# Edge sources and lanes read once in the mean pass of a four-layer graph network, instead of turn by turn

## The chip, the cores and the metric

The kernel runs on one core of a Trainium2 chip. The metric is the device time of one execution in microseconds (us), lower is better. A core has five engines with their own instruction streams: TensorE (PE in the profile, with its weight loads as PEld), VectorE (DVE), ScalarE (ACT), GpSimd (POOL) and SyncE (SP). They meet only at semaphores. SP and ACT issue plain DMAs, POOL issues the indirect ones (gathers).

## The reference

Four graph layers are applied in turn to `x`, 6,250 nodes of 96 numbers, over the same 200,000 edges, each with a source `src`, a target `dst` (the edges come sorted by `dst`), 32 attributes (`edge_attr_32`) and 17 attributes (`edge_attr_17`). Each layer adds its result to `x` and reads `h = relu(layernorm(x))`.

```
L0  out[d]  = mean over edges into d of (h[src] @ W + b)
L1  in      = [h[src], attr32];  msg = gelu(in@mW1+mb1)@mW2+mb2;  gate = sigmoid(gelu(in@gW1+gb1)@gW2+gb2)
    agg[d]  = sum of msg*gate;   out = layernorm(h + gelu([h,agg]@uW1+ub1)@uW2+ub2)
L2  w       = relu(attr17@W1.T+b1)@W2.T+b2;   agg[d] = sum of w*h[src];   out = relu(h@Ws.T+bs+agg@Wn.T+bn)
L3  three graph convolutions with degree-normalised sums, between two dense layers
```

## The kernel before

Nodes lie in 49 blocks of 128 (`NB`). The first stages bring the edges into a sorted form in the chip's memory and build a dense count matrix (`adjacency`); L0 (the mean pass, `mean_layer`) and L3 (`graph_layers`) multiply with it. L1 and L2 run through the edges themselves in `edge_pass`, once as `"gated"` (L1) and once as `"filter"` (L2). The change is about these two edge passes.

An edge tile is 128 consecutive edges of one node block. There are `T` = 1,612 of them, handled `G` = 4 at a time: a pass is `Q` = 403 turns. Rings have `GPI` = 6 slots of one turn each. For a turn the pass needs the first sorted row of each tile (`tile_row`, one number per tile), the (source, target) pairs of its 512 edges (`sorted_pairs` in HBM, `pairs_h`), their attributes (`sorted_attr`), and the node rows of the sources, gathered from `node_rows_wide` (192 numbers, gated) or `node_rows` (96 numbers, filter).

The function `turns` writes out the order of an engine by hand: every engine gets a list of (work, lag), and in its iteration n it does each work of turn n minus lag, in the order of the list. A program loop holds six iterations.

In the gated pass:

- SP (`load`, L1850s): waits until the consumers are done with the slot (`rows_used`, `src_kept`, `fields`: turn n-6), reads four row numbers into registers and issues four DMAs of pairs into `idx_ring` (L1858).
- POOL (`gather`, L1883): waits for the pairs (`idx_ready`), then issues four indirect DMAs into `rows`.
- ACT: `tanh` of turn n-5 (L1977), `gelu` of n-4 (L1972), `keep` of n-4 (L1982: copies the sources to `src_all`, for the filter pass), and then `load_attributes` of n: four row numbers and four DMAs into `attr_ring` (L1839).
- DVE: `dots` of n-3 (L2012), `combine` of n-2 (L2003, the only reader of the gathered `rows`), `gates` of n-3 (L2019), `turn_attrs` of n (L1995), and `hots_and_adds`: for turn n-3 it subtracts `tile_node` from the targets (L1907, gives `lane_all`), makes four one-hot tiles `hots` (L1917), and between them adds the four sums of turn n-4 into `accT` (L1926).
- PE: `edge_part` of n-1 (L1959), `sum_targets` of n-3 (L1932).

In the filter pass SP issues one DMA for the sources (`src_all` to `idx_ring`, L1861) and four for attributes (L1839); POOL gathers as before; PE does transposes of the attributes (`ps_t`, L1941, lag 0), `layer1` (`ps_e`, L2033, lag 1), `layer2` (`ps_w`, L2040, lag 2) and `sum_targets` (L1932, lag 4); ACT `keep_attrT` (L1948, lag 0) and `relu` (L2051, lag 1); DVE hots (L1920, lag 4) and adds (L1926, lag 5) and then `times` (L2060, lag 3, the only reader of `rows`).

PE and DVE depend on each other in each turn: `sum_targets` needs the one-hots (semaphore `hot`), the adds and the next one-hots need the sums (`summed`).

## Time and profile before

| | before |
|---|---|
| median of 3 runs | 8719.87 us (8703.91 to 8736.1) |
| the profiled execution, its own time | 8702.86 us |
| its span, first to last instruction | 8701.0 us |
| lies around the span | 1.9 us |
| mean granted TensorE clock | 0.749 of full speed |
| busy: PE / DVE / POOL / ACT | 67% / 50% / 37% / 20% |

The profile is one execution. "Busy" counts an engine's own work, not its register, branch and semaphore instructions or the issue of a DMA by SP or ACT; a gather counts as busy on POOL. An idle time is put down to what released it; "remote" and "issue" stand where no recorded instruction could be named as the releaser. Start times in a timeline are counted from the start of the span.

### The profile page before, as it was taken

Reading aid. Unit: us, or ns where it says so; the run is one execution under the profiler, and the core shown is the slowest. Engines: PE = TensorE matmul, PEld = TensorE weight load, DVE = VectorE, ACT = ScalarE, POOL = GpSimd, SP = SyncE. Lnnn points to the kernel's source line nnn. Section 1 sums busy time; section 2 is a strip of 40 time slices with the busy share of each in tenths; the row PEclk is TensorE's granted clock in tenths of the full one; section 3 lists DMA queues with packets and bytes.
Section 4 is the critical chain, followed back from the end, with each engine's and each line's share of the span. In section 5 each row is a group of like instructions: output and inputs, shape, how many; then the busy total and the mean of one; then the engine's idle time right before and its main releaser. Section 6 shows DMA issues by size and latency. Waiting matters only on the chain. (4 is left out here: it accounts for less than half of the span.)

```text
span 8701.0 us, 138050 instructions
## 1 busy us (share of the span) xinstructions
PE 5807.8 (67%) x29615; PEld 4088.1 (47%) x29617; DVE 4309.2 (50%) x14738; ACT 1723.7 (20%) x3202; POOL 3183.4 (37%) x3326
## 2 busy tenths in 40 slices
PE   4313666784455455555554688888888788889999
PEld 4312344663333333333332455555555555677777
DVE  7877888335666666666666333333333333332222
ACT  0013888101111111111111111111111111110000
POOL 0101000005555555555552455555555555300000
PEclk9956888897777777777777656655665666689999
DMA  1231333653333333333332211111111111256666
GB/s 31 101 100 60 105 106 107 215 180 77 68 71 69 70 70 67 71 69 70 71 70 31 42 34 35 34 35 34 35 34 34 33 36 35 24 188 252 249 243 221
DMA packets 1067041, 756.40 MB, mean 87 GB/s; under 512 B 870578, under 2 KB 979842, under 8 KB 1035091
## 3 DMA queue, kind: packets, MB, share of 16 engines
q1 hardware_dynamic: 679714, 476.62, 18.5%
q0 software_dynamic: 131296, 241.31, 10.9%
q10 hardware_dynamic: 255904, 37.09, 2.5%
q8 instruction: 43, 0.70, 0.0%
q14 instruction: 84, 0.68, 0.0%
HBM read 651.15 MB, written 141.61 MB: 91 GB/s over the span
## 5 line engine op out<-in xcount | busy, mean ns | idle before, releaser
L1883 POOL DMA_INDIRECT rows<-node_rows,idx_ring x1612 | 1529.2, 949 | 1215.1 <-DMA idx_ring<-src_all 702.5
L1883 POOL DMA_INDIRECT rows<-node_rows_wide,idx_ring x1612 | 1544.0, 958 | 1149.5 <-DMA idx_ring<-sorted_pairs 634.5
L1932 PE MATMUL ps_sum<-hots,act_ring 128*97 128x128 f32 x3224 | 657.8, 369 | 1326.6 <-DVE hots L1917 621.1
L1920 DVE TENSOR_SCALAR hots<-iota,lane_all 128x128 f32<-128x128 f32 x1612 | 461.6, 287 | 1820.4 <-remote 1283.4
L1932 PEld LDWEIGHTS ps_sum<-hots,act_ring 128*97 128x97 f32 x3224 | 556.7, 234 | 1618.9 <-DVE accT L1926 1235.1
L1932 PE MATMUL ps_sum<-hots,msg 128*96 128x128 f32 x3224 | 724.4, 399 | 419.0 <-DVE hots L1920 212.6
L1389 PE MATMUL ps_conv<-conv_rows,adj_ring 128*128 128x288 bf16 x7350 | 919.1, 287 | 29.8 <-PEq L1765 16.2
L1926 DVE TENSOR_TENSOR accT<-accT,ps_sum 97x128 f32 (+1 forms) x3224 | 905.8, 281 | 37.0 <-issue 16.0
L1932 PEld LDWEIGHTS ps_sum<-hots,msg 128*96 128x96 f32 x3224 | 624.9, 258 | 449.9 <-DVE accT L1926 360.2
L1959 PE MATMUL ps_e<-w1e,aT 128*128 128x384 f32 x1612 | 814.7, 642 | 18.3 <-DVE aT L1995 15.9
L1389 PEld LDWEIGHTS ps_conv<-conv_rows,adj_ring 128*128 128x128 f16 x7350 | 721.6, 98 | 212.1 <-issue 18.2
L2040 PEld LDWEIGHTS ps_w<-w2w,hid 97*128 97x128 f32 x3224 | 577.6, 269 | 516.1 <-issue 475.2
L2033 PE MATMUL ps_e<-aT,w 18*96 18x512 f32 x806 | 656.5, 906 | 55.6 <-ACT aT L1948 34.6
L2040 PE MATMUL ps_w<-w2w,hid 97*128 97x96 f32 x3224 | 661.5, 370 | 22.7 <-issue 12.0
L1125 DVE TENSOR_TENSOR end_hot<-iota_h,lanes 128x3072 bf16<-128x3072 bf16 x350 | 602.8, 1756 | 144.8 <-PE ps_blocks L1149 142.8
L1149 PE MATMUL ps_blocks<-end_hot 128*128 128x256 bf16 x2800 | 493.1, 323 | 256.3 <-POOLq L1196 191.2
L1948 ACT ACTIVATE aT<-ps_t 18x512 f32<-18x512 f32 x403 | 235.6, 585 | 2034.1 <-remote 1567.5
L1917 DVE TENSOR_SCALAR hots<-iota,lane_all,gate 128x128 f32<-128x128 f32 x1612 | 564.5, 352 | 17.1 <-issue 1.3
L1149 PEld LDWEIGHTS ps_blocks<-end_hot 128*128 128x128 bf16 x2800 | 304.0, 109 | 446.1 <-issue 347.6
L1977 ACT ACTIVATE th<-z,half_gb 128x4 f32<-128x4 f32 x403 | 119.8, 297 | 1897.6 <-remote 918.5
L1959 PEld LDWEIGHTS ps_e<-w1e,aT 128*128 128x128 f32 x1612 | 380.9, 261 | 195.4 <-issue 141.3
L2003 DVE TENSOR_TENSOR act_ring<-ps_e,rows 128x384 f32<-128x384 f32 x806 | 413.2, 548 | 64.5 <-issue 34.6
(345 smaller groups left out, 5907.2 us busy)
## 6 DMA issues: line engine op xcount, KB each, us to landing
adj_ring<-adjacency SPq DMA_DIRECT2D x240, 1280.0 KB, 5.5
adjacency<-panels SPq DMA_DIRECT2D x588, 128.0 KB, 1.7
attr_ring<-sorted_attr ACTq DMA_DIRECT2D x1612, 16.0 KB
idx_ring<-sorted_pairs SPq DMA_DIRECT2D x1612, 1.0 KB
rows<-node_rows_wide,idx_ring POOLq DMA_INDIRECT x1612
attr_ring<-sorted_attr SPq DMA_DIRECT2D x1612, 8.5 KB
rows<-node_rows,idx_ring POOLq DMA_INDIRECT x1612
sorted_attr<-in_edge_attr SPq DMA_DIRECT2D x5, 5000.0 KB
```

The costliest lines, as they stand in the source:

```text
L1125: v.tensor_tensor(end_hot[:, r, n * PAIRS:(n + 1) * PAIRS, :, :, :] .rearrange("p t c l k -> p (t c) l k"), iota_h[:, :, :].unsqueeze(1).t ...
L1149: pe.matmul(ps_b[:, dyn(at[j], WD)], src_hot[:, r, j // 2, :, j % 2], dst_hot[:, r, j // 2, :, j % 2], start=False, stop=True, skip_group_ ...
L1389: last = pe.matmul(ps[:, d, 0:width], ring[:, c, s * cols + d * P:s * cols + (d + 1) * P], nodes[:, c * CB + s, 0:width], start=(c == 0 an ...
L1883: g.indirect_dma_start(out=rows[:, r, j, 0:width], out_offset=None, in_=table, in_offset=bass.IndirectOffsetOnAxis(ap=idx, axis=0)).then_i ...
L1917: last = v.tensor_scalar(hots[:, r % 2, j, :], iota[:, :], lane, gate[:, r % 3, j:j + 1], ALU.is_equal, ALU.mult)
L1920: last = v.tensor_scalar(hots[:, r % 2, j, :], iota[:, :], lane, None, ALU.is_equal)
L1926: v.tensor_tensor(acc, acc, ps_sum[0:M, ra % 2, j, :], ALU.add).then_inc(added.sem, 1)
L1932: last = pe.matmul(ps_sum[0:M, r % 2, j, :], what(r, j), hots[:, r % 2, j, :], start=True, stop=True)
L1959: last = pe.matmul(ps_e[:, r % 2, c, 0:4 * D], aT[:, r % 2, :], w1e[:, 2 * c:2 * c + 2, :].rearrange("p j d -> p (j d)"), start=True, stop ...
L2003: last = v.tensor_tensor(act_ring[:, r % 3, 2 * c:2 * c + 2, :, 0:D].rearrange("p j a d -> p (j a) d"), ps_e[:, r % 2, c, 0:4 * D].rearran ...
L2033: pe.matmul(ps_e[0:D, r % 2, :], w17[:, :], aT[:, r % 2, :], start=True, stop=True).then_inc(edge_mm.sem, 1)
L2040: last = pe.matmul(ps_w[:, r % 2, j, 0:D], hid[:, r % 2, j * P:(j + 1) * P], w2w[:, :], start=True, stop=True)
```

## The change

Near the end of the mean pass the pairs of all 1,612 tiles are brought on chip once. SP spreads `tile_row` (padded to 13 x 128) over the partitions (`tile_at`), POOL gathers for each of 13 columns 128 tiles' pairs, 1 KB per tile (`pair_rows`), ACT casts them to float, PE turns them with 13 transposes for the sources and 13 for the targets, and ACT copies these out of PSUM to `src_all` and `lane_all` (four copies each). A DVE instruction in the stage that stores the wide rows turns `lane_all` into lanes for all tiles at once.

In both edge passes `idx_ring` is then filled by ACT: a new first work `take_sources` (lag 0) waits until the gathers of turn n-6 have landed and copies the turn's four columns of `src_all`. POOL waits for this copy and, itself now, for `rows_used`. SP issues attribute loads alone in both passes; the pair DMAs, the source DMAs, `keep`, `load_attributes` on ACT and the lane subtraction per turn are gone. In the filter pass the lags of all PE, ACT and DVE works grow by one.

```diff
@@ mean_layer @@
                 def _(sp):
+                    sp.dma_start(tile_at[:, :], tile_row[:, :].rearrange("o (p k) -> o p k", k=TC))\
+                        .then_inc(tile_at_in.sem, 16)
                     load_adjacency(sp, ring, 0, range(1, NK))
+                    sp.wait_ge(tile_at_in.sem, 16)
                 def _(g):
                     gather_heavy(g, heavy_rows)
+                    g.wait_ge(tile_at_in.sem, 16)
+                    for k in range(TC):
+                        g.indirect_dma_start(out=pair_rows[:, k, :], out_offset=None, in_=pairs_h,
+                                             in_offset=bass.IndirectOffsetOnAxis(ap=tile_at[:, k:k + 1], axis=0))\
+                            .then_inc(pairs_in.sem, 16)
+                @block.scalar
+                def _(a):
+                    a.wait_ge(pairs_in.sem, 16 * TC)
+                    a.activation(pair_rows[:, :, :].bitcast(F32).rearrange("p k e -> p (k e)"),
+                                 pair_rows[:, :, :].rearrange("p k e -> p (k e)"), ACT.Copy).then_inc(pairs_cast.sem, 1)
+                    for c, t in enumerate((src_all, lane_all)):
+                        by_run = t[:, :].rearrange("p (t n) -> p n t", n=TC)
+                        for n, (first, runs) in enumerate(quads):
+                            a.wait_ge(pairs_turned.sem, c * len(quads) + n + 1)
+                            a.activation(by_run[:, first:first + runs, :],
+                                         ps_p[:, n, 0:runs * P].rearrange("p (k t) -> p k t", t=P),
+                                         ACT.Copy).then_inc(pairs_kept.sem, 1)
                 def _(pe):
+                    def turn_pairs(c):
+                        for n, (first, runs) in enumerate(quads):
+                            if c:
+                                pe.wait_ge(pairs_kept.sem, n + 1)
+                            for k in range(runs):
+                                last = pe.transpose(ps_p[:, n, k * P:(k + 1) * P], pair_f[:, first + k, :, c], ident[:, :])
+                            last.then_inc(pairs_turned.sem, 1)
...
+                    multiply_panels(pe, ring, nodes, 3 * D + 2, ps, 0, (0,) * (NC - 1) + (1,), after)
+                    turn_pairs(1)
@@ edge_pass @@
-                def load_attributes(a, q, turn, r):
-                    past(a, rows_used, q - (GPI - 1))
-                    attributes(a, ACTE, q, r)
+                def take_sources(a, q, turn, r):
+                    if not isinstance(turn, int) or turn > 0:
+                        a.wait_ge(gathered[r].sem, base[gathered[r]] + turn * (16 * G))
+                        a.sem_inc(passed_a.sem, 1)
+                    a.activation(idx_ring[:, r, :], src_all[:, dyn(q * G, G)], ACT.Copy).then_inc(idx_ready[r].sem, 1)
...
                         past(sp, rows_used, q - (GPI - 1))
-                        if first:
-                            past(sp, src_kept, q - (GPI - 1))
-                            past(sp, fields, q - (GPI - 1))
-                            for j, row in enumerate(rows_of(q, SP)):
-                                sp.dma_start(idx_ring[:, r, j, :], pairs_h[dyn(row, P), :])\
-                                    .then_inc(idx_ready[r].sem, 16)
-                        else:
-                            sp.dma_start(idx_ring[:, r, :, 0], src_all[:, dyn(q * G, G)])\
-                                .then_inc(idx_ready[r].sem, 16)
-                        if kind == "filter":
-                            attributes(sp, SP, q, r)
+                        attributes(sp, SP, q, r)
...
-                        g.wait_ge(idx_ready[r].sem, base[idx_ready[r]] + (turn + 1) * (16 * (G if first else 1)))
+                        g.wait_ge(idx_ready[r].sem, base[idx_ready[r]] + turn + 1)
                         g.sem_inc(gather_go.sem, 1)
+                        past(g, rows_used, q - (GPI - 1))
+                        g.sem_inc(passed_g.sem, 1)
...
-                        if first:
-                            v.wait_ge(idx_ready[r].sem, base[idx_ready[r]] + (turn + 1) * (16 * G))
-                            cs = dyn(q * G, G)
-                            v.tensor_tensor(lane_all[:, cs], idx_ring[:, r, :, 1], tile_node[:, cs],
-                                            ALU.subtract).then_inc(fields.sem, 1)
-                            past(v, fields, q + 1)
@@ gated, ACT @@
-                        turns(a, [(tanh, 5), (gelu, 4), (keep, 4),
-                                  (lambda q, t, r: load_attributes(a, q, t, r), 0)])
+                        turns(a, [(lambda q, t, r: take_sources(a, q, t, r), 0), (tanh, 5), (gelu, 4)])
@@ filter, PE / ACT / DVE @@
-                        turns(pe, [(lambda q, t, r: transposes(pe, q, t, r, KB), 0), (layer1, 1), (layer2, 2),
-                                   (lambda q, t, r: sum_targets(pe, q, t, r, lambda r, j: msg[:, r % 3, j, :]), 4)])
+                        turns(pe, [(lambda q, t, r: transposes(pe, q, t, r, KB), 1), (layer1, 2), (layer2, 3),
+                                   (lambda q, t, r: sum_targets(pe, q, t, r, lambda r, j: msg[:, r % 3, j, :]), 5)])
-                        turns(a, [(lambda q, t, r: keep_attrT(a, q, t, r, KB, edge_mm), 0), (relu, 1)])
+                        turns(a, [(lambda q, t, r: take_sources(a, q, t, r), 0),
+                                  (lambda q, t, r: keep_attrT(a, q, t, r, KB, edge_mm), 1), (relu, 2)])
-                        turns(v, [(lambda new, old: hots_and_adds(v, new, old), 4, 5), (times, 3)])
+                        turns(v, [(lambda new, old: hots_and_adds(v, new, old), 5, 6), (times, 4)])
@@ keep_wide @@
+                chain(v, vec, v.tensor_tensor(lane_all[:, 0:T], lane_all[:, 0:T], tile_node[:, :], ALU.subtract))
```

## Rows read from the trace of the kernel before

**Rows 1.** Stages: PE, PEld, DVE, ACT, POOL busy us (count), granted clock, DMA share, GB/s.

```profile
1565.00:1901.00 336.00, 318.92 (x2548) 250.81 (x2548) 70.83 (x203) 11.35 (x15) 1.01 (x1) 0.97 0.69 247
...
1973.00:4690.00 2717.00, 1381.53 (x4836) 912.10 (x4836) 1673.20 (x8463) 494.49 (x1210) 1543.97 (x1612) 0.75 0.33 69
...
4811.00:7574.00 2763.00, 2245.66 (x8866) 1494.18 (x8866) 909.88 (x3625) 448.36 (x806) 1530.21 (x1614) 0.61 0.20 34
```

**Rows 2.** Page, costliest groups: count, busy us, mean ns, idle before and its releaser.

```profile
L1883 POOL DMA_INDIRECT rows<-node_rows,idx_ring x1612 | 1529.2, 949 | 1215.1 <-DMA idx_ring<-src_all 702.5
L1883 POOL DMA_INDIRECT rows<-node_rows_wide,idx_ring x1612 | 1544.0, 958 | 1149.5 <-DMA idx_ring<-sorted_pairs 634.5
...
L1948 ACT ACTIVATE aT<-ps_t 18x512 f32<-18x512 f32 x403 | 235.6, 585 | 2034.1 <-remote 1567.5
```

**Rows 3.** Instructions on the tile rows by stretch: DVE busy (count), POOL busy (count).

```profile
1973.00:3000.00 1027.00, 154.85 (x302) 587.73 (x615) 0.75 0.32 69
...
4811.00:6000.00 1189.00, 93.89 (x170) 664.00 (x701) 0.61 0.19 34
```

**Rows 4.** The tile rows: idle before its users, by releaser (us, times).

```profile
  DMA rows<-node_rows_wide,idx_ring: 4.2, 2
```

**Rows 5.** Waits in the gated pass: total us, times, longest.

```profile
ACT th L1977 <- remote: 918.5, 140, 11.9
POOL rows L1883 <- DMA idx_ring<-sorted_pairs: 629.8, 172, 7.8
...
DVE lane_all L1907 <- remote: 329.2, 127, 7.8
DVE gate L2019 <- issue: 260.1, 101, 8.9
```

**Rows 6.** Waits in the filter pass.

```profile
ACT aT L1948 <- remote: 1567.5, 186, 16.8
DVE hots L1920 <- remote: 1283.4, 182, 13.6
POOL rows L1883 <- DMA idx_ring<-src_all: 701.0, 174, 7.7
```

**Rows 7.** Timeline of the filter pass, PE: start, length, what.

```profile
6010.46 1.91 PE L1932 MATMUL ps_sum<-hots,msg 128*96 128x128 f32 x8
```

**Rows 8.** The same stretch, DVE.

```profile
6016.40 0.28 DVE L1920 TENSOR_SCALAR hots<-iota,lane_all 128x128 f32<-128x128 f32 x1 [7.58 <-remote]
```

**Rows 9.** The same stretch, POOL, first and last of eight gathers.

```profile
6006.67 0.94 POOL L1883 DMA_INDIRECT rows<-node_rows,idx_ring  x1 [2.51 <-issue]
...
6015.41 0.95 POOL L1883 DMA_INDIRECT rows<-node_rows,idx_ring  x1 [0.30 <-issue]
```

**Rows 10.** The same stretch and the next turn, SP issuing four attribute loads.

```profile
6011.17 5.04 SPq L1839 DMA_DIRECT2D attr_ring<-sorted_attr  x4
...
6019.81 1.95 SPq L1839 DMA_DIRECT2D attr_ring<-sorted_attr  x4
```

**Rows 11.** Timeline of the gated pass, DVE, from one transpose to the first one-hot.

```profile
3007.93 0.30 DVE L1995 STREAM_TRANSPOSE aT<-attr_ring 128x128 f32<-128x128 f32 x1
3008.37 0.16 DVE L1907 TENSOR_TENSOR lane_all<-idx_ring,tile_node 128x4 int32 x1
3008.57 0.35 DVE L1917 TENSOR_SCALAR hots<-iota,lane_all,gate 128x128 f32<-128x128 f32 x1
```

**Rows 12.** Gated pass, ACT issuing a turn's four attribute loads.

```profile
3008.64 0.32 ACTq L1839 DMA_DIRECT2D attr_ring<-sorted_attr  x1
...
3009.12 1.36 ACTq L1839 DMA_DIRECT2D attr_ring<-sorted_attr  x3
```

**Rows 13.** Start of the gated pass, POOL's first gather.

```profile
1977.70 0.99 POOL L1883 DMA_INDIRECT rows<-node_rows_wide,idx_ring  x1 [4.74 <-DMA idx_ring<-sorted_pairs]
```

**Rows 14.** Start of the filter pass, POOL's first gather and a turn's transposes.

```profile
4813.52 0.95 POOL L1883 DMA_INDIRECT rows<-node_rows,idx_ring  x1 [1.43 <-DMA idx_ring<-src_all]
...
4818.48 1.01 PE L1941 MATMUL ps_t<-ident,attr_ring 128*18 128x128 f32 x4 [2.05 <-DMA attr_ring<-sorted_attr]
```

More of the change, by code:

```diff
@@ L277, in graph_kernel @@
         gathered = [sem(f"gathered{k}") for k in range(GPI)]
-        src_kept = sem("src_kept")
-        fields = sem("fields")
+        tile_at_in = sem("tile_at_in")
+        pairs_in = sem("pairs_in")
+        pairs_cast = sem("pairs_cast")
+        pairs_turned = sem("pairs_turned")
+        pairs_kept = sem("pairs_kept")
+        passed_g = sem("passed_g")
         hot = sem("hot")
@@ L643, in graph_kernel @@
                 assert T + 4 * P <= 3 * (TP - COLS) // 2
-                row_f = tile_row[:, :].bitcast(F32)
+                row_f = tile_row[:, 0:T].bitcast(F32)
                 PC = T // 4
@@ L887, in take_rows @@
                     if half:
-                        link(v, v.tensor_scalar(tile_row[:, :], row_f, float(PADDED), None, ALU.min))
+                        step(v, v.memset(tile_row[:, T:TC * P], PADDED))
+                        link(v, v.tensor_scalar(tile_row[:, 0:T], row_f, float(PADDED), None, ALU.min))
                     else:
@@ L1483, in mean_layer @@
                 ps = ctx.enter_context(nc.psum_tensor("ps_mean", [P, 4, 512], F32))
+                ps_p = ctx.enter_context(nc.psum_tensor("ps_pairs", [P, 4, 512], F32))
                 block = ctx.enter_context(nc.Block("mean"))
+                pair_f = pair_rows[:, :, :].bitcast(F32).rearrange("p k (e c) -> p k e c", c=2)
+                quads = [(first, min(4, TC - first)) for first in range(0, TC, 4)]
                 @block.sync
                 def _(sp):
+                    sp.dma_start(tile_at[:, :], tile_row[:, :].rearrange("o (p k) -> o p k", k=TC))\
+                        .then_inc(tile_at_in.sem, 16)
                     load_adjacency(sp, ring, 0, range(1, NK))
+                    sp.wait_ge(tile_at_in.sem, 16)
                 @block.gpsimd
@@ L1802, in edge_pass @@
                 attr_ring = tmp("attr_ring", [P, GPI, G, EA if kind == "gated" else KB])
-                idx_ring = tmp("idx_ring", [P, GPI, G, 2 if first else 1], I32)
+                idx_ring = tmp("idx_ring", [P, GPI, G], I32)
                 if kind == "gated":
@@ L1818, in edge_pass @@
                     msg = tmp("msg", [P, 3, G, D])
-                base = {s: s.n for s in (idx_ready + attr_ready + gathered + [gather_go, fields, src_kept, hot, summed, added,
+                base = {s: s.n for s in (idx_ready + attr_ready + gathered + [gather_go, hot, summed, added,
                                                                 attrT, attrT_kept, edge_mm, edge_used, edge_act,
@@ L2061, in times @@
                                             ALU.mult).then_inc(edge_used.sem, 1)
-                        turns(v, [(lambda new, old: hots_and_adds(v, new, old), 4, 5), (times, 3)])
+                        turns(v, [(lambda new, old: hots_and_adds(v, new, old), 5, 6), (times, 4)])
                 for r in range(GPI):
                     uses = len(range(r, Q, GPI))
-                    idx_ready[r].n += 16 * uses * (G if first else 1)
+                    idx_ready[r].n += uses
                     attr_ready[r].n += 16 * uses * G
@@ L2071, in edge_pass @@
                 added.n += T
-                if first:
-                    fields.n += Q
-                    src_kept.n += Q
                 for s in (attrT_kept, edge_mm, edge_used, edge_act):
```

25 lines of the change are left out of this document (15 added, 10 removed).

## The prediction

> **What bounds the kernel now.** The views were read from the whole to the turn: busy time by stage, then the waits of each edge pass, then who uses the gathered rows, then a few microseconds of the timeline.
>
> The stages [rows 1] say where the change can act. The two edge passes take 2717 and 2763 us, 63% of the span, which is 6.74 and 6.86 us for each of 403 turns. No engine fills a turn: in the gated pass DVE is busy 4.15 us of 6.74, PE 3.43, POOL 3.83; in the filter pass PE 5.57 of 6.86 (at a granted clock of 0.61, so mostly at the lower of its two levels, 1.2 GHz), POOL 3.80, DVE 2.26. POOL's true need is larger than its busy time: gathers issued back to back start 1.25 us apart ([rows 9]: eight in 8.74 us between the first and last start), so four take 5.0 us, and 403 turns 2,015 us. This is the floor of a pass that only gathers.
>
> The page's costliest group [rows 2] points at the loads that the change removes: POOL idles 634.5 us for the pair DMAs and 702.5 us for the source DMAs. It is tempting to book these 1,337 us as the gain. Two views speak against it. First, who waits for the rows: all users of the gathered rows together waited for a landing 4.2 us, twice [rows 4]. Second, how far POOL is ahead. At 3000 us it has issued 615 gathers (153.75 turns) and DVE has done 302 instructions of two a turn (151 turns); at 6000 us 701 gathers (175.25 turns) against 170 turns [rows 3]. So rows lie ready 2.75 turns ahead in the gated pass and 5.25 of six slots ahead in the filter pass. POOL's idle time is that of an engine that is not the bottleneck.
>
> What is late is the talk between the others. In the gated pass ACT's tanh waits 918.5 us and DVE's lane step 329.2 us for "remote" [rows 5]; in the filter pass ACT's copy 1567.5 us and DVE's one-hots 1283.4 us [rows 6]. One case shows what that is. PE's `sum_targets` ends at 6012.37 (6010.46 + 1.91) [rows 7], but DVE, which waits for nothing else, goes on at 6016.40 [rows 8], 4.0 us later. In this time POOL issues eight gathers without a pause [rows 9], and SP needs 5.04 us for the four loads for which it needs 1.95 us in the next turn [rows 10]. I read it so: while gathers follow each other without a gap, semaphore updates and the sequencers of SP, ACT and DVE are slow, and they recover when POOL stops. The gathers' work is the same after the change, so this cost stays.
>
> **The change, part by part.** The sum is made against the profiled execution, 8702.86 us (span 8701.0 and 1.9 around it), which lies 17.0 below the median of 8719.87; the forecast is given on the scale of the median.
>
> (a) *Pair and source DMAs of SP become a copy on ACT.* SP loses four of four DMAs a turn in the gated pass and one of five in the filter pass, and gets the four attribute loads of the gated pass. For POOL the path from a free slot to its gather no longer has a DMA in it. Nobody waits for the rows, so I take 0. Bounds: all of POOL's waits come back, -1331 us (629.8 + 701.0, [rows 5, 6]); the other end is in (e).
>
> (b) *Lane step out of the gated turn.* From the end of the transpose (3007.93 + 0.30 = 3008.23) to the first one-hot (3008.57) pass 0.34 us, with the lane step of 0.16 in it and the wait on its own result [rows 11]. DVE's other neighbours follow one another at once, so 0.30 us go. DVE is the busiest of the engines that wait for each other, and the step lies in its chain whether the sums are early or late. 403 x 0.30 = -121 us. Bounds: the instruction alone, 403 x 0.16 = -64; the whole stretch, 403 x 0.34 = -137.
>
> (c) *Attribute loads leave ACT.* Issuing them takes ACT 1.84 us a turn (3008.64 to 3010.48) [rows 12]. Before, they stood between `gelu` and the next `tanh`. ACT's own work is 494.49 / 403 = 1.23 us a turn, so with 1.84 it comes to 3.1 of 6.74: it is not full. DVE's waits for the gate without a named releaser sum up to 260.1 us [rows 5], and behind them stands tanh, which itself waited for "remote". I take 0, bounds -260 and 0. On SP the four loads replace four DMAs of the same kind (both are DMAs from a register address), its queue holds nothing else, and their slot comes free four turns before use; 0.
> The Trainium skill ("DMA: Bandwidth & Descriptors", section "Issuing engines are not separate DMA queues") says that DMAs of different issuers run on the same engines and that a second issuer saves only issue time. By it, putting both queues into one costs or gains nothing but the 1.84 us a turn of ACT's issue time, -742 us if ACT were the path and 0 if not. The rows here show more than that: the issue time itself is 1.95 or 5.04 us by what POOL does.
>
> (d) *Mean pass.* 13 gathers (13 x 1.25 = 16 us on an idle POOL), the cast and eight copies on an idle ACT (585 ns for 512 columns [rows 2]) lie under 336 us of panels, but the last copies don't. PE is busy 319 of 336 us [rows 1], so its 26 transposes count in full: the nearest row has four in 1.01 us [rows 14], 26 x 0.25 = 6.6 us; the last target copy adds 0.6, and DVE's last panel runs beside that. +6, bounds 3 and 12. The lanes' subtraction (128 x 1612) runs beside a product of PE: 0, at most 2. The padding of `tile_row` is one small instruction.
>
> (e) *The new order in the filter pass.* `take_sources` of turn n stands behind `relu` of n-3, and that needs `layer1` of n-3, which PE reaches only after `sum_targets` of n-7. So the copy comes a few microseconds after `times` of n-6 frees the slot, where the source DMA came about 3 us after it. POOL is 5.25 turns ahead, so I take 0. The bound is in the second rival: +262. ACT's copy itself (some 0.2 us beside 448.36 / 403 = 1.1 us busy) is hidden by ACT's long waits.
>
> (f) *Starts.* The first gather of the gated pass began 4.74 us after the instruction before it [rows 13], that of the filter pass waited 1.43 us [rows 14]. -5, bounds -6 and 0.
>
> Sum: -121 + 6 - 5 = -120, or 8583 against 8702.86, and **8600** on the scale of the median, -1.4%. A turn of the gated pass would take 6.44 us, one of the filter pass 6.86.
>
> **The rivals.**
>
> *Rival 1, the passes speed up as a whole.* POOL's pauses also end the slow phases; if the pauses come after each turn (5 us of gathers) instead of two (10 us), semaphores are late for a smaller part of the time, and ACT without DMAs answers sooner. For it: 1,337 us of POOL's idle time hang on the removed DMAs, and 742 us of issue time leave ACT. Against it: [rows 3, 4]. The floor is 5.0 us a turn on POOL and 5.57 on PE at its present clock. If a third of POOL's 1331 us comes back: 8600 - 444 = 8156; with a fifth 8330.
>
> *Rival 2, slower.* Place: the filter pass, where POOL's restart hangs on (e). Two turns are gathered in one go, so there are some 201 restarts. If each comes 1.3 us later than now and the rest of the turn waits along (because PE and DVE get their semaphores only when the run of gathers ends), that is +262 us: 8600 + 262 = 8862. In the gated pass the like can happen the other way: POOL, no longer held up by SP, issues three or four turns in one go, and the slow phase grows by as much. The sign flips against (b) from 0.6 us per restart on (121 / 201). For it: in [rows 7, 8] the release comes near the end of the run of gathers. Against it: POOL's lead of 5.25 turns [rows 3].
>
> *Rival 3, no change.* DVE's 0.30 us are swallowed: each turn of the gated pass ends when the late semaphore comes, and DVE waits that much longer (329.2 us before the very step, [rows 5]). Then 8720 + 1 = 8721.
>
> **How the numbers follow.** Chances: the forecast 0.40, Rival 1 0.25, Rival 2 0.23, Rival 3 0.12. What a measurement of this kernel can tell from no change is 0.5%, 44 us. The forecast's own range, by the bounds of (b), (c), (d) and (f), is 8340 to 8665, most of it near the upper end. Range for 8 in 10: from 8250 (half of Rival 1 left out) to 8830 (the upper part of Rival 2 left out). Faster by over 0.5%: the forecast, nearly all of Rival 1 and none of the others, less a part of the forecast that ends above 8676, 0.60. Within 0.5%: Rival 3 and the mild ends, 0.16. Slower: 0.24.
>
> **What would show it.** Right: the gated pass near 6.4 us a turn and the filter pass near 6.9; POOL's waits on `idx_ring` gone from the list, but its idle time still there, now before `rows_used`; "remote" waits of ACT and DVE as long as before; the mean pass 6 us longer. Rival 1: both passes under 6.3 us a turn, with runs of four gathers. Rival 2: runs of 12 gathers and more, the filter pass over 7.1. The prediction fails if the late semaphores do not come from the gathers but from the DMAs of SP and ACT, of which the gated pass loses half: then the gated pass alone would fall to about 6 us.

## The result, and the profile after

The changed kernel takes 8751.63 us (median of 6 runs, 8740.13 to 8767.62), the kernel before 8717.21 on the same chip: 1.0041 of before, 95% interval 1.0026 to 1.0056. It is slower by some 34 us where 8600 was forecast. The profiled execution has a span of 8748.9 us, 47.9 more than before.

In groups and counts, the change did what it says. Stages of the kernel after, as [rows 1] (mean pass, gated pass, filter pass):

```profile
1565.00:1911.00 346.00, 325.46 (x2580) 254.81 (x2577) 70.99 (x203) 19.52 (x23) 13.41 (x14) 0.96 0.70 244
...
1981.00:4767.00 2786.00, 1257.39 (x4812) 828.67 (x4812) 1581.73 (x8017) 497.54 (x1207) 1529.65 (x1613) 0.74 0.29 67
...
4899.00:7627.00 2728.00, 1927.79 (x8861) 1302.05 (x8862) 909.33 (x3623) 494.46 (x1209) 1522.43 (x1614) 0.69 0.21 34
```

The mean pass is 10 us longer (346 for 336), the gated pass 69 (2786 for 2717), the filter pass 35 shorter (2728 for 2763). DVE's 403 lane steps of 0.16 us are gone from the gated pass, and it is longer all the same.

The page's groups of the gathers, as [rows 2]:

```profile
L1924 POOL DMA_INDIRECT rows<-node_rows_wide,idx_ring x1612 | 1529.5, 949 | 1243.0 <-ACT idx_ring L1890 760.9
L1924 POOL DMA_INDIRECT rows<-node_rows,idx_ring x1612 | 1521.4, 944 | 1188.5 <-issue 614.4
```

POOL's idle time in the gated pass is 1243.0 for 1149.5: the wait for SP's DMAs is gone from the list and stands there under ACT's copy. The users of the gathered rows, as [rows 4], waited even less for a landing:

```profile
  DMA rows<-node_rows_wide,idx_ring: 0.9, 1
```

Waits of the gated pass (first fence, as [rows 5]) and of the filter pass (second, as [rows 6]): total, times, longest.

```profile
ACT th L2012 <- DVE z L2041: 1305.9, 183, 16.7
...
DVE hots L1952 <- remote: 782.2, 111, 10.8
POOL rows L1924 <- ACT idx_ring L1890: 760.9, 143, 8.4
```

```profile
DVE hots L1955 <- remote: 1170.3, 155, 13.0
ACT aT L1983 <- remote: 1144.5, 155, 10.5
...
POOL rows L1924 <- ACT idx_ring L1890: 570.5, 155, 5.0
```

DVE, which waited 329.2 us for "remote" before its lane step, now waits 782.2 before the one-hots that follow it. In the filter pass both "remote" waits fell, by 113 and 423 us.

For a finer account I take the starts in the timeline of each pass's first gather and first and last `sum_targets` on PE (with its first weight load); "us a turn" is from here on the time from the first to the last sum, by 402. A run is a string of gathers that start less than 1.45 us apart; the pause behind it is the time to the next gather beyond the usual 1.25 us.

| | before | after | difference |
|---|---|---|---|
| end of the mean pass (DVE's last `x`) | 1901.1 | 1911.2 | +10.0 |
| from there to the first gated gather | 76.6 | 74.2 | -2.3 |
| first gated gather to first sum | 14.1 | 25.7 | +11.6 |
| gated, 402 turns | 6.703 a turn | 6.875 | +69.4 |
| last gated sum to first filter gather | 127.2 | 126.7 | -0.5 |
| first filter gather to first sum | 35.2 | 30.9 | -4.3 |
| filter, 402 turns | 6.773 a turn | 6.701 | -28.9 |
| the rest | 1129.6 | 1122.5 | -7.1 |

Runs of gathers: gated mean 7.1 before (146 of 228 runs have 8) and 9.2 after (88 of 176 have 12); filter 7.3 before (161 of 221 have 8) and 4.5 after (302 of 361 have 4). The mean pause behind a run of the gated pass is 2.89 us before and 4.29 after.

One run of 12 in the gated pass after, with what DVE, ACT and PE do about it:

```profile
3011.89 0.94 POOL L1924 DMA_INDIRECT rows<-node_rows_wide,idx_ring  x1 [4.84 <-ACT idx_ring L1890]
...
3016.46 1.88 PE L1967 MATMUL ps_sum<-hots,act_ring 128*97 128x128 f32 x8
...
3025.63 0.95 POOL L1924 DMA_INDIRECT rows<-node_rows_wide,idx_ring  x1 [0.30 <-issue]
3028.42 0.34 DVE L1952 TENSOR_SCALAR hots<-iota,lane_all,gate 128x128 f32<-128x128 f32 x1 [9.98 <-issue]
...
3032.43 0.84 ACT L2007 ACTIVATE act_ring<-act_ring 128x768 f32<-128x768 f32 x1 [0.64 <-DVE act_ring L2032]
...
3033.18 0.19 ACT L1890 ACTIVATE idx_ring<-src_all 128x4 int32 x1
...
3034.31 0.94 POOL L1924 DMA_INDIRECT rows<-node_rows_wide,idx_ring  x1 [7.74 <-ACT idx_ring L1890]
```

PE's sum ends at 3018.34. DVE, which needs it for the next one-hots, goes on at 3028.42, 10.1 us later and 2.79 us after the start of the run's last gather. The row says "issue": the trace has no release just before DVE goes on, so it doesn't tell whether the semaphore was late or DVE's own sequencer. It wasn't semaphores alone: SP's recorded instructions, which start 0.06 to 0.37 us apart from 3009.01 to 3012.41, start 0.7 or 1.4 us apart (but for one) from 3016.15 to 3028.95, and 0.02 to 0.37 us apart again until 3030.32. "Late semaphore" stands below for a hand-over that comes late, whichever of the two it is. Then the consumers still need one-hots, `dots`, `combine`, `gelu` and the copy before POOL may gather again: 5.9 us more.

### The profile page after: what moved, and what is told of

The parts are those of the page before. It is cut to its first block and busy times, and to the rows that moved or that the text cites. A ratio compares the mean times of both kernels' runs of the same rounds, so it can differ in the third digit from the quotient of the medians.

```text
span 8748.9 us, 133287 instructions
## 1 busy us (share of the span) xinstructions
PE 5386.9 (62%) x29641; PEld 3824.5 (44%) x29643; DVE 4227.6 (48%) x14337; ACT 1783.9 (20%) x3614; POOL 3173.4 (36%) x3339
## 5 line engine op out<-in xcount | busy, mean ns | idle before, releaser
L1924 POOL DMA_INDIRECT rows<-node_rows_wide,idx_ring x1612 | 1529.5, 949 | 1243.0 <-ACT idx_ring L1890 760.9
L1967 PE MATMUL ps_sum<-hots,act_ring 128*97 128x128 f32 x3224 | 599.4, 345 | 1523.3 <-DVE hots L1952 658.0
L1955 DVE TENSOR_SCALAR hots<-iota,lane_all 128x128 f32<-128x128 f32 x1612 | 479.1, 299 | 1787.1 <-remote 1170.3
L1967 PEld LDWEIGHTS ps_sum<-hots,act_ring 128*97 128x97 f32 x3224 | 504.9, 214 | 1793.7 <-DVE accT L1961 1303.0
L1967 PE MATMUL ps_sum<-hots,msg 128*96 128x128 f32 x3224 | 651.7, 369 | 778.9 <-DVE hots L1955 748.9
L1952 DVE TENSOR_SCALAR hots<-iota,lane_all,gate 128x128 f32<-128x128 f32 x1612 | 554.9, 345 | 986.6 <-remote 782.2
L1967 PEld LDWEIGHTS ps_sum<-hots,msg 128*96 128x96 f32 x3224 | 558.1, 234 | 806.3 <-DVE accT L1961 791.3
L1994 PE MATMUL ps_e<-w1e,aT 128*128 128x384 f32 x1612 | 746.5, 596 | 18.9 <-DVE aT L2024 15.9
L2069 PEld LDWEIGHTS ps_w<-w2w,hid 97*128 97x128 f32 x3224 | 474.6, 226 | 402.0 <-issue 385.6
L2062 PE MATMUL ps_e<-aT,w 18*96 18x512 f32 x806 | 550.7, 768 | 2.8 <-ACT aT L1983 2.1
L2069 PE MATMUL ps_w<-w2w,hid 97*128 97x96 f32 x3224 | 548.6, 323 | 4.1 <-issue 4.1
L1994 PEld LDWEIGHTS ps_e<-w1e,aT 128*128 128x128 f32 x1612 | 351.7, 242 | 177.9 <-issue 110.8
```

Of the source, the lines that this page charges most:

```text
L1924: g.indirect_dma_start(out=rows[:, r, j, 0:width], out_offset=None, in_=table, in_offset=bass.IndirectOffsetOnAxis(ap=idx, axis=0)).then_i ...
L1952: last = v.tensor_scalar(hots[:, r % 2, j, :], iota[:, :], lane, gate[:, r % 3, j:j + 1], ALU.is_equal, ALU.mult)
L1955: last = v.tensor_scalar(hots[:, r % 2, j, :], iota[:, :], lane, None, ALU.is_equal)
L1967: last = pe.matmul(ps_sum[0:M, r % 2, j, :], what(r, j), hots[:, r % 2, j, :], start=True, stop=True)
L1994: last = pe.matmul(ps_e[:, r % 2, c, 0:4 * D], aT[:, r % 2, :], w1e[:, 2 * c:2 * c + 2, :].rearrange("p j d -> p (j d)"), start=True, stop ...
L2062: pe.matmul(ps_e[0:D, r % 2, :], w17[:, :], aT[:, r % 2, :], start=True, stop=True).then_inc(edge_mm.sem, 1)
```

## The experiments

The first four kernels ran on a chip where the kernel before takes 8689.41 us. The next twelve ran on three chips where the same kernel takes 7308 to 7317 us, and the last two on one where it takes 8654.37. Chips that take near 8700, that of the result among them, are the first kind here, the others the second; no chip among them showed both times. All ratios are to the kernel before on the same chip.

### First kind: the lane step, and where ACT's copy stands

**e1_lane_back**

```diff
 def hots_and_adds(...):                    # gated pass
+    v.tensor_tensor(lane_all[:, cs], lane_all[:, cs], tile_node[:, cs], ALU.subtract).then_inc(fields.sem, 1)
+    past(v, fields, q + 1)
 def keep_wide(...):
-    chain(v, vec, v.tensor_tensor(lane_all[:, 0:T], lane_all[:, 0:T], tile_node[:, :], ALU.subtract))
```

> Kernel after, with the lane subtraction put back into each turn of the gated pass (and taken out of the stage that stores the wide rows). Theory A, run length: the step taken out of the turn was worth its 0.30 us, and the gated pass lost more than that because POOL now issues 12 gathers in one go; then putting the step back makes the gated pass 0.2 to 0.3 us a turn longer, 2870 to 2905 us instead of 2786, and the kernel 8830 to 8870. Theory B, swallowed: the step lay in time that DVE waits anyway; the gated pass stays at 2786 within 20 us and the kernel at 8750.

**e2_gated_lag3** and **e3_gated_lag5**: `(tanh, 4), (gelu, 3)` and `(tanh, 6), (gelu, 5)` in place of `(tanh, 5), (gelu, 4)` on ACT.

> Kernel after, gated pass only: ACT's gelu has lag 3 instead of 4 and tanh 4 instead of 5, so the copy of a turn's sources stands behind gelu of n-4 instead of n-5 and POOL is at most 4 turns ahead. Theory A, run length: POOL's runs shrink from 12 gathers to 8 or 4, and the gated pass falls from 6.9 to 6.4 to 6.7 us a turn (2600 to 2700 us instead of 2786). Theory B, swallowed: run length is of no account, 2786 within 20. Theory C, lead: POOL's lead is what covers the late semaphores, so a turn less of it makes DVE wait for rows and the pass goes above 7.0 us a turn (over 2840).

> Kernel after, gated pass only: gelu has lag 5 and tanh 6, so the copy stands behind gelu of n-6 and holds POOL back no more; POOL waits for the free slot alone. Theory A, run length: runs of 12 gathers or more, the gated pass 2786 to 2900 us. Theory C, lead, or a theory that ACT's copy is late for POOL: the pass gets faster, under 2740. Theory B: 2786 within 20.

**e4_filter_lag5**: `(keep_attrT, 4), (relu, 5)` in place of `(keep_attrT, 1), (relu, 2)` on ACT.

> Kernel after, filter pass only: keep_attrT has lag 4 and relu 5 instead of 1 and 2, so the copy of sources comes three turns earlier against the rest of ACT's work and POOL is held by the free slot alone. Theory A, run length: runs grow from 4 gathers to 8 or 12 and the filter pass from 2728 to 2780 to 2880 us. Theory B: 2728 within 20, whatever the runs are.

| kernel | ratio (95%) | gated us a turn | mean run | filter us a turn | mean run |
|---|---|---|---|---|---|
| before | 1 | 6.70 | 7.1 | 6.77 | 7.3 |
| after | 1.0041 (1.0026 to 1.0056) | 6.88 | 9.2 | 6.70 | 4.5 |
| e1_lane_back | 0.9926 (0.9901 to 0.9951) | 6.62 | 7.1 | 6.69 | 4.5 |
| e2_gated_lag3 | 1.0051 (1.0030 to 1.0072) | 6.85 | 9.0 | 6.72 | 4.8 |
| e3_gated_lag5 | 1.0050 (1.0022 to 1.0079) | 6.87 | 9.5 | 6.69 | 4.6 |
| e4_filter_lag5 | 1.0321 (1.0292 to 1.0351) | 6.87 | 9.8 | 7.26 | 7.5 |

With the lane step back, DVE does more and the kernel is faster than both others. The gated pass gets 0.25 us a turn shorter (against 6.87 in e4, whose gated pass is that of the kernel after, on the same chip), and POOL's runs fall back to a mean of 7.1 (79 runs of 4, 75 of 8, 39 of 12). Theory A said longer, theory B the same; neither has the sign. The gated pass of e1_lane_back, in which DVE's records sum up to 1664.20 us of work for 1581.73 after the change:

```profile
1984.00:4680.00 2696.00, 1320.94 (x4840) 866.07 (x4840) 1664.20 (x8463) 499.12 (x1209) 1539.16 (x1612) 0.75 0.29 69
```

How late DVE's hand-over from PE is can be measured turn by turn: from the moment when PE's sum has ended and DVE is free, to DVE's next instruction (the lane step where there is one, the first one-hot else). In the gated pass this is on average 1.09 us a turn before the change, 2.44 after it, and 1.53 with the lane step back. Of the kernel after, 128 of the 402 turns lose over 2.5 us there, of e1_lane_back 93. The turn adds up in the same way from POOL's side: mean pause by turns in a mean run is 2.89 / 1.77 = 1.63 us before, 4.29 / 2.29 = 1.87 after and 2.82 / 1.77 = 1.59 in e1_lane_back, and with four gathers, 5.0 us, this gives 6.6, 6.9 and 6.6. So a run that is a third longer had a pause behind it that is half as long again.

Where ACT's copy stands in the gated pass changes next to nothing (e2, e3: the turn moves by 0.03 us at most, mean runs are 9.0 and 9.5; theory A of e2 forecast shorter runs and 6.4 to 6.7). In the filter pass it does: e4 goes up by 0.56 us a turn. There the runs are as long as before the change, but the turn is 0.49 us longer than before. So run length goes with the time within a pass and doesn't set it alone. The timeline of e4 shows one cycle of two turns:

```profile
6000.01 0.94 POOL L1924 DMA_INDIRECT rows<-node_rows,idx_ring  x1 [4.93 <-DVE msg L2090]
...
6003.87 1.04 PE L1967 MATMUL ps_sum<-hots,msg 128*96 128x128 f32 x8
...
6004.74 0.60 PE L1976 MATMUL ps_t<-ident,attr_ring 128*18 128x128 f32 x4
...
6008.76 0.95 POOL L1924 DMA_INDIRECT rows<-node_rows,idx_ring  x1 [0.30 <-issue]
6011.59 0.29 DVE L1955 TENSOR_SCALAR hots<-iota,lane_all 128x128 f32<-128x128 f32 x1 [8.54 <-remote]
6011.61 0.59 ACT L1983 ACTIVATE aT<-ps_t 18x512 f32<-18x512 f32 x1 [7.91 <-remote]
...
6013.24 0.55 DVE L2090 TENSOR_TENSOR msg<-ps_w,rows 128x384 f32<-128x384 f32 x1
...
6014.57 0.95 POOL L1924 DMA_INDIRECT rows<-node_rows,idx_ring  x1 [4.87 <-DVE msg L2090]
```

PE's sum ends at 6004.91 and its transposes at 6005.34. DVE waits for the one, ACT for the other, and both go on at 6011.6, 2.8 us after the last gather of the run has started. Here it is the semaphores that are late: the trace has their updates at 6011.45 and 6011.51, over 6 us after PE's work. In this pass that is the rule: of the 201 times that DVE waited more than 2.5 us for its one-hots, 180 ended 2.47 to 2.97 us after the start of a run's last gather. It is not the rule elsewhere. In the gated pass of the kernel after, 11 of 128 such waits end in that band and 38 end while the run still goes on; in [rows 8, 9] the wait ends 0.99 us after the last start. The cycle then adds up: 8.75 us from first to last gather, 2.83 to the late semaphore, 1.65 to `times`, 1.33 to POOL's restart, 14.56 in all or 7.28 a turn (7.26 measured). What a turn costs is thus the four gathers, 5.0 us, and the pause after a run shared over its turns. That the pause is long or short by which semaphore of the consumers' chain was caught in the run is my reading of such cycles; no run tests it.

### Second kind: no late semaphores, and POOL is the bound

The next eleven kernels ran on the second kind, so the parts of their expectations that are about late semaphores weren't tested there.

**e5_pause** (gated), **f1_pause_both** and **g1_short_pause** (both passes, 1024 and 512 columns, and with the lags of e4 in the filter pass):

```diff
 def gather(q, turn, r):
     for j in range(G): ...
+    past(g, paused, q)
+    g.memset(idle_at[:, :], 0.0).then_inc(paused.sem, 1)
```

> Kernel after, gated pass only: behind the four gathers of each turn POOL clears a scratch tile of 128 x 1024 (estimated at 0.9 us by the memset of 1 x 1024 in the kernel after, 946 ns), so no run of gathers can be longer than 4. Theory A, run length: a turn's four gathers and the pause take 6.0 us, and with late semaphores for only a short part of each run the pass takes 6.1 to 6.6 us a turn (2460 to 2660 us instead of 2786). Theory D, the number of gathers: semaphores are late for as long as POOL works, however it is spread; then the pass stays at 6.9 us a turn or gets longer by the pause (up to 7.9).

> Kernel after with a pause of 0.95 us (a memset of 128 x 1024 on POOL) behind the four gathers of each turn in both passes, and in the filter pass also keep_attrT at lag 4 and relu at lag 5, the setting that made that pass 7.26 us a turn on the first chip (8 gathers in one go) and that the pause should break up. On a chip with late semaphores (kernel before near 8700). Theory A, run length: runs of 4 in both passes, gated 6.1 to 6.6 us a turn instead of 6.88, filter 6.1 to 6.8 instead of 7.26. Theory D, semaphores are late for as long as POOL works: gated 6.9 or more, filter 7.2 or more. On a chip without them (kernel before near 7314): 5.0 + 0.95 = 5.95 us a turn in both, by either theory.

> Kernel after with a pause on POOL of a memset of 128 x 512 (0.4 to 0.5 us, half of the one of 128 x 1024) behind each turn's four gathers in both passes, and in the filter pass keep_attrT at lag 4 and relu at 5. On a chip with late semaphores. Theory A, run length: runs of 4, gated 5.8 to 6.6 us a turn instead of 6.88, filter 5.8 to 6.8 instead of 7.26. Theory D, semaphores are late as long as POOL works: gated 6.8 or more, filter 7.2 or more. On a chip without: 5.0 + 0.45 = 5.45 us a turn in both by POOL's work alone.

**e6_filler**, run again as **f2_filler**: `v.tensor_tensor(filler, iota[:, 0:G], iota[:, 0:G], ALU.subtract)` in the place of the lane step. **e7_lane_twice**: e1_lane_back with the step twice.

> Kernel after, with one DVE instruction of the lane step's size (128 x 4, about 0.1 us) on a scratch tile put into each turn of the gated pass, where the lane step stood, with no wait on its result. The lane step put back made the pass 0.26 us a turn shorter. Theory E, phase: any small delay between the transpose and the one-hots shifts when POOL's slots come free and breaks up the runs of 12; then the pass falls from 6.88 to 6.6 to 6.75 us a turn. Theory F: it is the wait on the step's own result (or the subtraction of all lanes in the other stage) that counts; then it stays at 6.88 within 0.05.

> Kernel after with the lane step put back twice a turn, each with the wait on its own result (0.6 us of DVE's chain instead of 0.3). Theory E, phase: runs of gathers get no longer than with one step (mean 7.1) and the gated pass is 6.5 to 6.75 us a turn; beyond the first, the second costs or gives less than 0.15. Theory G, the chain counts as soon as runs are short: 0.3 us more than with one step, 6.92.

**e8_one_gather**, **f3_fewer_gathers**, **g2_two_three**: `for j in range(GG)` in `gather`, with `rows` of the other tiles set to zero once. These kernels leave out the sources of those tiles, so their times show what a turn costs with fewer gathers and nothing more.

> Kernel after, gated pass only: one gather a turn instead of four; the rows of the other three tiles of a turn are zeros, so a part of the computation is left out (the sources of three edge tiles in four). All DMAs of SP, all copies and all sums stay. Theory A and D alike, gathers make the semaphores late: no late semaphores, and the pass falls to DVE's own work, 3.9 us a turn and at most 4.6 (1570 to 1850 us instead of 2786). Rival, the DMAs that SP issues or the PE clock set the turn: it stays above 6 us.

> Kernel after with one gather a turn in the gated pass and two in the filter pass; the rows of the other tiles are zeros, so the sources of three tiles in four and of two in four are left out of the computation. On a chip with late semaphores, theory A (gathers back to back make them late, at least three in a row): gated 3.9 to 4.6 us a turn, as on the chip without (3.94), and filter 4.0 to 5.2. If the chip's semaphores are late whatever POOL does: gated stays above 6.

> Kernel after with two gathers a turn in the gated pass and three in the filter pass; the rows of the other tiles are zeros (sources of two tiles in four and of one in four left out of the computation). On a chip with late semaphores, theory A: gated 3.9 to 5.0 us a turn instead of 6.88, since two in a row never made a semaphore late, filter 4.5 to 6.0 instead of 6.70. Rival, a cause outside the gathers: gated above 6. On a chip without: gated 3.94 (the time with one gather a turn, set by the other engines), filter 3.75 to 3.85 by POOL's three gathers.

**f4_after_again** and **h1_before**: the changed kernel and the kernel before, unchanged.

> The changed kernel itself. On a chip with late semaphores (before near 8700): 1.003 to 1.006 of before, gated 6.88 and filter 6.70 us a turn. On a chip where POOL's gathers follow one another without a pause (before near 7314): both passes 5.0 us a turn by POOL's four gathers, whatever the other engines save, so within 0.5% of before: 0.998 to 1.003.

> The kernel before, unchanged, for its trace. On a chip without late semaphores (7314): both passes bound by POOL's gathers, 5.0 to 5.1 us a turn; the 16 us that the changed kernel gains are then made up of a gain of some 25 us in the gated pass (lane step, ACT's loads) less 10 us in the mean pass; if instead the gated pass is equal, the gain lies at the passes' starts. On a chip with late semaphores (near 8700): 6.7 and 6.8 us a turn as in the trace shown.

| kernel | ratio (95%) | gated us a turn | filter us a turn |
|---|---|---|---|
| h1_before | 1 | 5.09 | 5.00 |
| f4_after_again | 0.9978 (0.9968 to 0.9989) | 5.06 | 5.00 |
| e6_filler, f2_filler | 0.9977, 0.9981 | 5.06 | 4.99 |
| e7_lane_twice | 1.0016 (1.0007 to 1.0026) | 5.12 | 4.99 |
| e5_pause | 1.0470 (1.0453 to 1.0488) | 5.97 | 4.99 |
| f1_pause_both | 1.0934 (1.0916 to 1.0952) | 5.96 | 5.82 |
| g1_short_pause | 1.0422 (1.0392 to 1.0453) | 5.43 | 5.41 |
| gathers a turn: e8 1 and 4, f3 1 and 2, g2 2 and 3 | | 3.94, 3.94, 4.01 | 5.00, 3.41, 3.74 |

Here all 1,612 gathers of the filter pass are one run, 1.25 us apart. Of f4_after_again, the two passes, and the filter pass's waits of DVE and POOL:

```profile
1975.00:4025.00 2050.00, 1292.64 (x4829) 814.52 (x4830) 1603.45 (x8056) 499.02 (x1209) 1538.41 (x1612) 0.82 0.39 90
4150.00:6181.00 2031.00, 1867.32 (x8861) 1254.88 (x8862) 925.05 (x3623) 513.60 (x1207) 1526.83 (x1612) 0.75 0.28 46
```

```profile
DVE msg L2090 <- DMA rows<-node_rows,idx_ring: 709.6, 313, 4.8
POOL rows L1924 <- issue: 488.2, 1602, 0.3
```

No "remote" wait of the kind in [rows 6] is among the large ones; DVE waits for the rows, POOL for nothing but the 0.3 us between gathers. In the gated pass of this kernel and of h1_before, the hand-over from PE's sum to DVE that costs 1.09 and 2.44 us a turn on the first kind costs 0.00. The pause is paid nearly in full: the memset of 0.97 us costs 0.91 us a turn in the gated pass and 0.83 in the filter pass, the one of 0.54 us 0.37 and 0.42. With fewer gathers the passes fall to 3.94 and 3.41 us: that is what the other engines need when POOL isn't in their way. The change gains 16 us by the medians. The two traced executions, on different chips, differ by 7.2 us: the 402 gated turns give 10.5, less than half of the 25 that were expected, and the mean pass, its new work included, costs 0.6 where 10 were expected.

### First kind again: the pause, fewer gathers, and the pair gathers spread out

**i3_pause_two** (this one on the second kind: 5.96 and 3.39 us a turn) and **j2_pause_two**, the same kernel: the pause of e5_pause in the gated pass and two gathers a turn in the filter pass.

> Kernel after; in the gated pass a memset of 128 x 1024 on POOL (0.95 us) behind each turn's four gathers; in the filter pass two gathers a turn instead of four (the rows of the other two tiles are zeros, left out of the computation). On a chip with late semaphores (before near 8700). Theory A, run length: gated 6.0 to 6.6 us a turn instead of 6.88; filter 3.5 to 4.5 instead of 6.70. Theory D, semaphores are late in proportion to POOL's gathering: gated 6.8 or more, filter about 4.5 to 5.5. A cause outside the gathers: filter above 6. On a chip without (before near 7314): gated 5.95, filter 3.41, as measured there.

> The same kernel as i3_pause_two: in the gated pass a pause of 0.95 us behind each turn's four gathers, in the filter pass two gathers a turn (the rows of the other two tiles are zeros, left out of the computation). On a chip with late semaphores: run length sets the turn, gated 6.0 to 6.6 us instead of 6.88; semaphores late in proportion to gathering, 6.8 or more; filter 3.5 to 4.5 us if two gathers in a row make nothing late, over 6 if the cause isn't in the gathers. On a chip without: 5.95 and 3.41.

**j1_spread**: e1_lane_back, and in the mean pass

```diff
     for k in range(TC):
+        if k:
+            g.wait_ge(adj_used.sem, k * NC * 11 // 12)
         g.indirect_dma_start(out=pair_rows[:, k, :], ...)
```

> Kernel after with the lane step back in the gated turn and with the 13 pair gathers of the mean pass one by one, each behind a share of the panels instead of all in a row under the first panel. On a chip with late semaphores (before near 8700): the mean pass ends at 1901 to 1904 instead of 1911, the gated pass takes 6.62 us a turn, in all 0.991 to 0.993 of before. If the gathers in a row aren't what delayed the first panel, the mean pass ends near 1911 still and the ratio is that of the lane step alone, 0.9926. On a chip without (before near 7314): no panel was delayed there, the mean pass ends within 2 us of the one in a row, and the ratio is 0.998 to 1.001.

Gated and filter pass of j2_pause_two, on a chip where the kernel before takes 8654 us:

```profile
1985.00:4423.00 2438.00, 1412.16 (x4834) 894.24 (x4835) 1757.03 (x8056) 496.02 (x1207) 1938.58 (x2015) 0.75 0.33 76
4548.00:5977.00 1429.00, 1404.20 (x8864) 964.46 (x8865) 909.31 (x3623) 512.01 (x1207) 774.96 (x806) 0.97 0.25 38
```

The gated pass, complete in what it computes, takes 6.02 us a turn in place of 6.87: an instruction of 0.97 us that does nothing for the result saves 0.85. (6.87 is from the other chip of the first kind; the two agree to 0.03, by the gated passes of e1_lane_back, 6.62, and j1_spread, 6.59. No kernel after without the pause was run on this chip.) Its POOL timeline:

```profile
3008.30 0.97 POOL L1940 MEMSET idle_at<- 128x1024 f32 x1
3009.43 0.95 POOL L1934 DMA_INDIRECT rows<-node_rows_wide,idx_ring  x1 [0.16 <-POOL idle_at L1940]
...
3013.22 0.95 POOL L1934 DMA_INDIRECT rows<-node_rows_wide,idx_ring  x1 [0.31 <-issue]
3014.17 0.96 POOL L1940 MEMSET idle_at<- 128x1024 f32 x1
3015.29 0.95 POOL L1934 DMA_INDIRECT rows<-node_rows_wide,idx_ring  x1 [0.16 <-POOL idle_at L1940]
```

The turn is now POOL's own, four gathers and the pause: 5.86 us from 3009.43 to 3015.29. Semaphores are still late in part (DVE waits 492.2 us for "remote", 187 times, at most 5.2; the hand-over from PE's sum costs 1.41 us a turn where it cost 2.44), but the wait mostly ends inside the turn. The same data moves in less time than in the kernel after (76 GB/s for 67, by the stage rows), so the lateness doesn't follow the rate of the data. With two gathers a turn the filter pass takes 3.50, next to 3.39 to 3.41 on the second kind. So the late semaphores come with gathers that follow one another: with half the gathers the filter pass is nearly free of them (7 hand-overs to its one-hots over 1 us late, 165 in the kernel after), and a gap after every fourth takes most of their cost away.

j1_spread takes 0.9946 of before (0.9923 to 0.9968), 8598.38 us, a little more than the 0.991 to 0.993 expected. It doesn't beat e1_lane_back by what can be told from the two intervals. But the mean pass ends at 1903.4, as expected if the gathers in a row delayed it, and its first panel is repaired. PE in it, kernel after and then j1_spread:

```profile
1593.99 14.49 PE L1396 MATMUL ps_mean<-mean_rows,adj_ring 128*128 128x290 bf16 x99 [13.83 <-PEq L1810]
...
1609.50 0.66 PE L1396 MATMUL ps_mean<-mean_rows,adj_ring 128*128 128x290 bf16 x4 [1.02 <-issue]
1611.63 0.68 PE L1396 MATMUL ps_mean<-mean_rows,adj_ring 128*128 128x290 bf16 x3 [1.48 <-issue]
```

```profile
1594.34 33.90 PE L1397 MATMUL ps_mean<-mean_rows,adj_ring 128*128 128x290 bf16 x260 [8.44 <-PEq L1813]
```

In the kernel after PE comes to a halt again and again while POOL issues its 13 gathers (1597.36 on). DVE takes the first pair of blocks at 1626.93, against 1618.43 before, 1619.15 in j1_spread and 1617.41 in f4_after_again on the second kind.

## Why the prediction was wrong

The forecast was 8600 and the median is 8752; the profiled span shows +47.9 where the sum said -120. Step by step:

- **(b), the step that failed**: "403 x 0.30 = -121 us", from "the step lies in its chain whether the sums are early or late". Put back, the step makes the gated pass 0.25 us a turn *shorter*, so taking it out cost some 101 us (0.25 x 402). The sum took DVE's chain as what sets the turn. On neither kind does the step's time pass through to it. On the first, the turn is the gathers and the pause behind a run; POOL's runs have a mean of 7.1 and a mean pause of 2.82 us with the step (e1_lane_back), 9.2 and 4.29 without. On the second, POOL's 5.0 us are the floor: a step costs 0.03 (e7 has two, +0.06). What e1_lane_back puts back is the step, the wait on its result, and the taking out of the one subtraction elsewhere, together; which of them counts wasn't separated on the first kind.
- **Rival 2** had the place and the form right for the gated pass ("POOL, no longer held up by SP, issues three or four turns in one go, and the slow phase grows"), but not the cause: POOL isn't held by SP or by the copy (e2, e3), and with the step back the runs are short although SP's DMAs are gone. Its main place, the filter pass, went the other way. Rival 3, swallowed, says 0 for the step and 8721 in all. That is the nearest of the four numbers to 8752, but by luck: it has neither the gated pass (+69 us) nor the filter pass (-29) in it.
- **(a) and (c)**, 0: e1_lane_back has them and keeps the lane step in the turn. It is 64 us faster than before (0.74% of 8689); the parts outside the gated pass give 33 of that by the table of the result, so I estimate that some 31 are left for (a) and (c) in the gated pass. By the traces, from its first gather to its last sum, that pass is 20 us shorter than before, on another chip. Which of the two gives them wasn't tried. The bounds of -1331 and -260 were far off, as the argument from the rows' users said. By the Trainium skill ("DMA: Bandwidth & Descriptors", section "Issuing engines are not separate DMA queues") a second issuer saves only issue time. The runs agree that putting both queues into one cost nothing that shows: of the 742 us of issue time that left ACT at most these 31 show in the time.
- **(d)**, +6: +10.0, of which the first panel's delay is 8.5. That wasn't in the sum at all: I priced the 13 gathers on an idle POOL and left out what I had read in [rows 10], that other engines are slow meanwhile. The transposes, which I took for the whole price, run at 1.71 us for 13 where 3.3 was estimated.
- **(e)**, 0: -29 over the turns, with runs of four. The copy behind `relu` holds POOL back in each turn (e4 takes that away, runs go to 8, and it costs 0.56 us a turn), much like the pause.
- **(f)**, -5: -2.3 and -0.5, and then +11.6 and -4.3 to the first sum. POOL's first run of the gated pass has 32 gathers where it had 16, so the first turns see late semaphores at once; with the pause the first sum comes 15.2 us after the first gather instead of 25.7 (j2_pause_two).
- The bounds of (b), (c), (d) and (f) give 8320 to 8668 for the forecast's own range; the 8340 to 8665 in the text is a slip that changes nothing.

What I read right is the source of the lateness: semaphores are late while gathers follow one another. What I read wrong is that "this cost stays" since the number of gathers stays. The cost hangs on how they are spaced, and that was the one thing that the lane step, the copy behind `relu` and the 13 gathers in a row all moved. My failure clause looked for the cause in SP's and ACT's DMAs; j2_pause_two has all of SP's loads and is 0.85 us a turn faster.

Open: why 0.3 us on DVE move the runs from 12 back to 4 and 8; a filler of 0.12 us was tried on the second kind alone, where POOL has next to no pauses. Open is also whether it is POOL's issuing of a gather or something in its transfer that slows the other engines. Open too is what makes a chip of one kind or the other. A complete kernel with the pause in both passes wasn't run on the first kind; from 6.02 for 6.87 in the gated pass alone I estimate 340 us less there. On the second kind the pause in the gated pass costs 359 us (e5_pause, 7658.23, against f4_after_again, 7299.56, on the same chip).

## What to carry to other kernels

An engine that issues gathers back to back can, on some chips, slow the hand-overs between the other engines, so its idle time may be what lets them work, and its bursts are worth spacing before any of their instructions is removed. When consumers wait for late semaphores, take no instruction of theirs at its duration: put it in and out and read how the bursts change. And ask on how many chips a gain was measured: the same change is 1.0041 on one kind and 0.9978 on the other, and the pause saves 0.85 us a turn on one and costs 0.91 on the other.

## What the runs showed of the hardware

- The same kernel takes 8654, 8689 and 8717 us on chips of one kind, and 7308 to 7317 on chips of the other. The part behind the last sum of the filter pass doesn't differ (1122.5 us after the change on the first kind, 1129.3 on the second); nearly all of the difference lies in the two passes of gathers (6.88 and 6.70 us a turn against 5.06 and 5.00).
- On the first kind, hand-overs caught in a run of gathers can come 10.1 us after the work that gives them (3018.34 to 3028.42). In the filter pass of e4, 180 of DVE's 201 long waits ended 2.47 to 2.97 us after the start of the run's last gather, once to two engines at once (6011.59 and 6011.61); in other passes many ended earlier, inside the run.
- In such a run SP's instructions start 0.7 or 1.4 us apart instead of 0.06 to 0.37 (kernel after, 3016.15 to 3028.95). In f4_after_again on the second kind, from 3011.03 to 3028.21, they are 0.06 to 0.43 us apart but for one wait a turn, under gathers that never stop.
- PE is slowed in a stretch where it only multiplies and takes in plain loads: 8.5 us lost beside 13 gathers in a row, 0.7 when they are spread out (j1_spread), none on the second kind (1617.41).
- The granted clock of the filter pass went from 0.61 to 0.69 with PE busy 318 us less, and the pass got 35 us shorter: PE was not its bound.
